# A backward segment-max scan that reads its maxima from PSUM, with transposes and features moved behind a tile's sums

## What is computed

```python
m = jax.ops.segment_max(e, dst, num_segments)      # e = edge_attr @ W_fcr.T
ex = jnp.exp(e - m[dst])                           # softmax numerators
denom = jax.ops.segment_sum(ex, dst, num_segments)
agg = segment_sum(ex / denom[dst] * (z[src] + e), dst)
```

## Time and profile before

| | |
|---|---|
| Median of 3 runs | 10931.24 us (10926.27 to 10934.09) |
| The profiled execution, its own time | 10930.99 us |
| Its span in the trace | 10929.1 us |
| POOL busy | 8175.2 us, 75% of the span |
| PE, DVE, ACT busy | 36%, 35%, 4% |
| TensorE clock granted, mean | 0.618 |

### The profile page before, as it was taken

One profiled execution on the slowest core, in us unless ns is written; L12 is line 12 of the kernel. 1 busy time (PEld: TensorE's weight loads), 2 busy tenths in 40 slices (PEclk: granted clock), 3 DMA queues, 4 the chain that ended last, 5 costly groups with the idle time before them and its releaser, 6 DMA issues.

```text
span 10929.1 us, 84376 instructions
## 1 busy us (share of the span) xinstructions
PE 3899.8 (36%) x18630; PEld 3008.6 (28%) x18631; DVE 3852.7 (35%) x4123; ACT 476.7 (4%) x740; POOL 8175.2 (75%) x8343
## 2 busy tenths in 40 slices
PE   1323333334444444222222224555555532222222
PEld 1212112223333333211111113554555521111111
DVE  4333333343443444354444432333333321222221
ACT  0000000011111111000000000000000000000000
POOL 4777777777777777777777777777777767777777
PEclk8666666666676666555555556777777755555555
DMA  4444344444554554312333312333333322222222
GB/s 101 112 108 114 100 105 114 108 133 149 150 155 141 160 156 137 88 39 55 62 63 62 63 39 60 81 81 77 84 81 81 81 45 42 42 42 42 42 42 40
DMA packets 712000, 950.46 MB, mean 87 GB/s; under 512 B 289345, under 2 KB 504385, under 8 KB 709453
## 3 DMA queue, kind: packets, MB, share of 16 engines
q0 software_dynamic: 266240, 385.62, 17.4%
q10 hardware_dynamic: 208528, 441.95, 13.5%
q1 hardware_dynamic: 236931, 119.79, 3.8%
HBM read 739.75 MB, written 206.15 MB: 87 GB/s over the span
## 4 chain that ended last, share of the span: by engine, by line
POOL 74%; issue 23%; DVE 1%; DMA 1%; PE 1%; SPq 0%; ACT 0%; DVEq 0%; ACTq 0%; POOLq 0%
POOL flat L283 74%; DMA flat<-table,stage 0%; DMA table<-flat 0%; PE pair L926 0%; SPq L297 0%; PE flip L997 0%; DMA wbd<-in_wfcr 0%; DVE flat L383 0%; DVE flat L381 0%; DVE flat L376 0%; DVE hk L375 0%; DVE flat L367 0%; DVE hk L366 0%; DVE dinv L368 0%; DVE has L364 0%
## 5 line engine op out<-in xcount | busy, mean ns | idle before, releaser
L283 POOL DMA_INDIRECT flat<-table,stage x8320 | 8170.5, 982 | 2736.8 <-issue 2532.3
L926 PE MATMUL pair<-flat 128*128 x9760 | 1610.0, 339 | 5649.3 <-SPq L334 5142.5
L926 PEld LDWEIGHTS pair<-flat 128*128 x9760 | 1173.5, 132 | 6130.5 <-issue 6067.8
L1080 PE MATMUL pair<-flat 128*128 x4880 | 1156.8, 408 | 949.2 <-DVE flat L686 949.0
L418 DVE TENSOR_TENSOR flat<-fixed,dcol 128x1024 f32 x915 | 1078.2, 1217 | 1164.5 <-PE pair L926 1032.8
L1080 PEld LDWEIGHTS pair<-flat 128*128 128x128 f32 x4880 | 1077.3, 247 | 1021.3 <-issue 1018.5
L460 DVE TENSOR_REDUCE batch<-pair 128x65 f32<-128x195 f32 (+1 forms) x392 | 140.3, 358 | 2908.9 <-PE pair L951 2908.9
L418 DVE TENSOR_TENSOR flat<-fixed,flat 128x1024 f32 x305 | 362.6, 1221 | 735.8 <-PE pair L926 680.9
L669 DVE TENSOR_TENSOR flat<-flat (+1 forms) x208 | 143.9, 692 | 1261.2 <-SPq L334 1261.2
L940 PE MATMUL wide<-flat,wbd 128*128 128x512 f32 x840 | 533.6, 787 | 135.6 <-DMA flat<-gate_d 102.1
L686 DVE TENSOR_TENSOR flat<-fixed,dcol 128x512 f32<-128x512 f32 x610 | 392.8, 683 | 40.1 <-DVE fixed L411 20.2
(11 more groups left out here) (142 smaller groups left out, 1809.8 us busy)
## 6 DMA issues: line engine op xcount, KB each, us to landing
flat<-table,stage POOLq DMA_INDIRECT x8320
flat<-in_ea ACTq DMA_DIRECT2D x140, 768.0 KB, 6.4
ex_d<-flat ACTq DMA_DIRECT2D x140, 768.0 KB, 5.2
flat<-ex_d SPq DMA_DIRECT2D x208, 512.0 KB
flat<-gate_d ACTq DMA_DIRECT2D x280, 192.0 KB, 7.3
pm_d<-flat ACTq DMA_DIRECT2D x70, 768.0 KB, 4.3
flat<-pm_d ACTq DMA_DIRECT2D x70, 768.0 KB
sort_d<-flat ACTq DMA_DIRECT2D x14, 1024.0 KB, 4.0
```

The source lines that it names most:

```text
L283: pool.indirect_dma_start(out=to_row, out_offset=None, in_=tables[p], in_offset=bass.IndirectOffsetOnAxis(ap=stage[:, st, c:c + 1].bitcast ...
L926: mm = M(bank[a % 2][:, 0:width], flat[:, ds(at_one[k], P * 2)].bitcast(bf16), flat[:, ds(at_row[k], TW * 2)].bitcast(bf16)[:, 0:width], s ...
L1080: mm = M(bank[a % 2][:, 0:F3], ohf[not first][:, k, :], exr[:, ds(g % XR, 1), k, :].rearrange("p o c -> p (o c)"), start=first and k == 0, ...
```

## The change

`ScalarE` gets a new operation, `maxima`: it copies the forward maxima `pm[h]` of a step from SBUF into `eh` in PSUM. The backward scan then reads `eh` in place of `pm[h]`. As `eh` is now occupied until the scan has read it, `features` comes after the scan. On VectorE the subtract and the multiply move behind the next tile's one-hots and the tile's sums. On TensorE the order in a tile becomes: sums, the turns of the step of the tile before, features. ScalarE loads two steps ahead, after a step's stores.

```diff
 # VectorE, stage 1, a tile with a step
                         dve.wait_ge(b_carry, st)
+                        dve.wait_ge(b_pm, st + 1)
                         dve.wait_ge(b_xe, st)
-                        V.tensor_tensor_scan(mx[:, ::-1], gate[h][:, ::-1], pm[h][:, ::-1],
+                        V.tensor_tensor_scan(mx[:, ::-1], gate[h][:, ::-1], eh[:, ::-1],
                                              carry[:, :], ALU.add, ALU.max).then_inc(b_scan, 1)
                         dve.wait_ge(b_scan, st + 1)
                         V.tensor_copy(carry[:, :], mx[:, 0:1]).then_inc(b_carry, 1)
+                    if a7 < B7 - 1:
+                        ga = hots(s1, N1, i, a + 1, ga, 0, build(s1, a + 1, dcol))
+                    sums_out(s1, t, a, F3)
+                    if a7 in AT:
                         dve.wait_ge(b_mm, st + 1)
                         V.tensor_tensor(pm[h], eh, mx, ALU.subtract).then_inc(b_sub, 1)
                         dve.wait_ge(b_ex, st + 1)
                         dve.wait_ge(s1["flip_full"], i * (2 * U1) + (hb * U1 + AT.index(a7) * NB))
                         V.tensor_tensor(xe, eh, pm[h], ALU.mult).then_inc(b_xe, 1)
-                    if a7 < B7 - 1:
-                        ga = hots(s1, N1, i, a + 1, ga, 0, build(s1, a + 1, dcol))
-                    sums_out(s1, t, a, F3)
 # ScalarE, stage 1
+            def maxima(st):
+                act.wait_ge(b_ld[st % 2], 64 * (st // 2 + 1))
+                act.wait_ge(b_xe, st)
+                S.activation(eh, pm[st % 2], ACT.Copy).then_inc(b_pm, 1)
             load_b(0)
+            load_b(1)
+            maxima(0)
...
-                    if st + 1 < STEPS:
-                        act.wait_ge(s1["flip_full"], u0)
-                        act.wait_ge(b_scan, st)
-                        load_b(st + 1)
                     act.wait_ge(b_sub, st + 1)
                     S.activation(pm[h], pm[h], ACT.Exp).then_inc(b_ex, 1)
+                    if st + 1 < STEPS:
+                        maxima(st + 1)
...
+                    if st + 2 < STEPS:
+                        load_b(st + 2)
 # TensorE, stage 1
-                    if a7 in AT:
-                        ...
-                        pe.wait_ge(b_xe, st)
-                        settle(pe)
-                        features(h).then_inc(b_mm, 1)
                     ga = tile_sums(1, i, a, ga, 0, summing(s1, a, F3))
-                    if a7 in AT:
-                        pe.wait_ge(b_xe, st + 1)
+                    if a7 - 1 in AT:
+                        n = hb * NS + AT.index(a7 - 1)
+                        h = n % 2
+                        pe.wait_ge(b_xe, i * (2 * NS) + (n + 1))
                         ... (the six blocks of turns, now of tile a7 - 1)
+                    if a7 in AT:
+                        ...
+                        pe.wait_ge(b_scan, st + 1)
+                        settle(pe)
+                        features(h).then_inc(b_mm, 1)
```

More of the change, by code:

```diff
@@ L194, in gnn_kernel @@
         b_ld = [sem(f"b_ld{h}") for h in range(2)]
-        b_mm, b_scan, b_carry, b_sub, b_ex, b_xe = [sem(n) for n in "b_mm b_scan b_carry b_sub b_ex b_xe".split()]
+        b_pm, b_mm, b_scan, b_carry, b_sub, b_ex, b_xe = [sem(n) for n in "b_pm b_mm b_scan b_carry b_sub b_ex b_xe".split()]
         b_st = [sem(f"b_st{h}") for h in range(2)]
@@ L978, in _ @@
                     hb, a7 = a // B7, a % B7
-                    if a7 in AT:
-                        n = hb * NS + AT.index(a7)
-                        st, h = i * (2 * NS) + n, n % 2
-                        pe.wait_ge(b_ld[h], i * (64 * NS) + 64 * (n // 2 + 1))
-                        settle(pe)
-                        pe.wait_ge(b_xe, st)
-                        settle(pe)
-                        features(h).then_inc(b_mm, 1)
                     ga = tile_sums(1, i, a, ga, 0, summing(s1, a, F3))
-                    if a7 in AT:
-                        pe.wait_ge(b_xe, st + 1)
+                    if a7 - 1 in AT:
+                        n = hb * NS + AT.index(a7 - 1)
+                        h = n % 2
+                        pe.wait_ge(b_xe, i * (2 * NS) + (n + 1))
                         for j in range(NB):
-                            u = hb * U1 + AT.index(a7) * NB + j
+                            u = hb * U1 + AT.index(a7 - 1) * NB + j
                             settle(pe)
@@ L999, in _ @@
                             mm.then_inc(s1["flip_full"], 1)
+                    if a7 in AT:
+                        n = hb * NS + AT.index(a7)
+                        st, h = i * (2 * NS) + n, n % 2
+                        pe.wait_ge(b_ld[h], i * (64 * NS) + 64 * (n // 2 + 1))
+                        settle(pe)
+                        pe.wait_ge(b_scan, st + 1)
+                        settle(pe)
+                        features(h).then_inc(b_mm, 1)
                     if a7 == B7 - 1:
```

## The result

The changed kernel takes 10774.05 us (median of 4 runs, 10772.83 to 10774.69), against 10930.5 for the kernel before (4 runs, 10926.27 to 10934.09). The ratio is 0.9855, 95% interval 0.9843 to 0.9868. That is 156.5 us less; 10772 was forecast, with 10756 to 10802 as the range. The profiled execution took 10772.83 us, its span is 10770.8.

The account below looks back on a forecast made before the run. POOL, issuing gathers back to back, was taken as the bound, with 70 gathers stretched beside stage 1's backward scans. 10930.99 - 169.2 + 5.5 + 5 = 10772 us, range 10756 to 10802.

Parts of the forecast that it names:

- stretched gathers beside scans: Stage 1: the stretching of 70 gathers beside backward scans goes, -169.2 us, bounds 0 and -172.7.
- end of stage 1: Turns of step 69 now precede the last transposes, so POOL waits longer: +5.5 us, bounds +3 and +7.
- batch ends: Stage 1's vector operations at 14 batch ends meet gathers at other moments: +5 us, bounds 0 and +25.
- ring: TensorE stays within the ring's 80 us in stage 1, so POOL is not held: cost 0.
- stage 1 in all: From stage 1's first gather to stage 2's: about 2113 us.
- if writing descriptors were all: At the scans: if gathers only wrote descriptors, the scan would not hold them and the change would give nothing.
- its minimum is 16: Stage 1's serial loop through `eh`: 14.1 us, about 16 with hand-overs, as a step's minimum.
- the loop above has 3 us to spare: Stage 1's loop through `eh` closes with 3 us to spare at rows' 21.2 us a tile.
- the load is late next: Stage 1: loads land at E+18, after the multiply's E+14.5, so `maxima` waits for the load.
- The second rival: Stage 1: steps over 24 us hold POOL through the ring; at 25.5, +101 us, 10873; chance 0.06.
- The fourth rival: Stage 1: the loop through `eh` becomes the bound; at 30 us a step, +220 us, 11151; chance 0.03.

Follow-up runs that it names:

- the copies: Changed kernel plus three fp32 copies of xe to idle mx in each of 70 steps: 13039.7 us, ratio 1.0078, in the machine's other condition.
- The nine copies: Changed kernel with each of ScalarE's 70 copies done nine times over: 11228.88 us, ratio 1.0279 to the kernel before; 1.0365 in the machine's other condition.
- the old order: Kernel before with the backward scan's operand in PSUM and turns and loads as before: 10758.84 us, ratio 0.9851; 1.0086 in the machine's other condition.
- the kernel that copies the keys: Changed kernel with steps on tiles 0 to 4, and ScalarE copying half the keys to PSUM for stage 2's 171 min/max pairs: 10668.19 us, ratio 0.9768.

## Why the prediction was right

**The bound and the mechanism** held. POOL's gathers are the bound, the scan stretched 70 of them, and the forward scan's rows foretold that one input in PSUM ends it. Term by term:

| term | forecast | measured |
|---|---|---|
| stretched gathers beside scans | -169.2 | -170.1 (170.4 to 0.3) |
| end of stage 1 | +5.5 | +4.8 (22.38 to 27.16) |
| batch ends | +5, 0 to 25 | +3.9 (2.2 to 6.1) |
| ring | 0 | 0.9 more wait in the whole run |
| stage 1 in all | 2113 | 2112.5 |

Another +2.0 is a thousandth of a us more in each of the other gathers of the stage. Start, stage 0 and stage 4 moved by -4.2, +3.3 and +1.8 and about cancel. None of these four was forecast, so that the total is met to 2 us is in part luck. The terms of the sum were each met to about 1 us.

**The clause of the Trainium skill**, "SBUF — State Buffer", section "SBUF: two separate sides", that two SBUF inputs hold out only a GpSimd operation that reads SBUF, would have given no gain if gathers only wrote there. The runs decide for practical purposes: an indirect DMA is held by a two-input operation. What it is doing when held was not put to a test, but the two places say something of it. A gather reads its row numbers from SBUF (`stage`, among its inputs in every row), and a two-input operation holds it only near its start, with 0.75 to 0.82 us to go. That fits a reading that is held, and then the clause is not contradicted: it is the forecast's "if writing descriptors were all" that is not met. The same section of the Trainium skill gives descriptor generation as what a copy in a two-port mode holds. It agrees with the copies' 0.37 us each and with their second place, 0.12 us before a gather's end.

**One step was wrong, and the sum didn't hang on it.** It is "its minimum is 16", and with it "the loop above has 3 us to spare". The 16 left the load out of the loop, though the same paragraph had found that the load is late next. Steps in a row need 20 to 21 us, so the room is 0.6 to 1.0 us a step and not 5. The time came out right because rows at 21.2 us are still slower than that, and POOL waited only 2.7 us for the ring. The second rival's count of 24 us a step as the limit was near but high in its effect: by it a batch at 32.5 us a step takes 190.5 us, and measured are 182.6 (2578.2 less 22.4 for a stage's end, over 14). The nine copies were underestimated through the step's length, not through the rule. The fourth rival, slower, had a chance of 0.03. In the machine's other condition the change is slower, but no trace shows that it is by late loads, as that rival has it.

## What to carry to other kernels

Where GpSimd issues indirect DMAs back to back, read the longest of them and not the mean, and look at which VectorE operation ended 0.75 to 0.82 us, or 0.12 us, before each one's end. Moving one of two SBUF operands to PSUM with idle ScalarE costs 1.45 us there and gave back 2.4 us for each scan, and another 89 us in the sort. Do that with the least change of order: the old order did at least as well. When a resource gets a second use, write out the loop through it with every load in it, because the room left decides how much more a step can carry.

## What the runs showed of the hardware

- An indirect DMA of 128 rows takes POOL 0.944 us, with 0.30 between two. Beside a scan of 3.41 us with two SBUF tensors one of them takes up to 4.07 us and ends 0.75 us after the scan. Those that are stretched start 0.1 to 1.3 us after the scan's start; one that is under way when a scan starts is not held by it (57 cases, none over 1.13 us). By the longest stretch, 3.1 of the scan's 3.41 us, the hold begins some 0.3 us into the scan, an estimate.
- Beside other vector operations with two SBUF tensors a held gather ends 0.82 us after the operation: 281 gathers of the kernel before. With one of the two in PSUM none is held: not by the forward scans, the backward scans of the changed kernel, or the sort's pairs of the kernel that copies the keys, nor by the one-hots, whose `fixed` lies in PSUM (306 of 1.22 us in stage 1).
- Fp32 copies SBUF to SBUF of 128x1536 take 0.97 us, where the multiply takes 1.76, and stretch gathers too, as does the 1.29 us multiply of 128x2048 by a column. Most gathers that they hold (91 of 133 beside the copies) end 0.12 us after them.
- One chip ran the kernel before in 10918 us and, in a later session, in 12952. The change was 1.4% faster in one condition and 1.1% slower in the other. The cause of the condition is open: the gathers' own time and the landing of their data are as usual, and the traces lack three quarters of the semaphore events.
